# Another order of blocks on TensorE in a fused attention and expert layer: the fourth up block and both shared down products among the scores, three expert products moved

## What is computed

```
xl = layernorm(layernorm(x));  c = layernorm(ctx)            # latents and context
q = xl @ W_q ; k, v = [c ; xl] @ W_kv                         # 4 heads of 64, 333 keys
q, k = rmsnorm(q) * q_gamma / 8, rmsnorm(k) * k_gamma
x1 = x + softmax(mask(q k^T)) v @ W_out + b_out
h  = layernorm(x1)
route: sigmoid(h @ gate^T), the better of 2 groups of 4 experts, its top 2, weights normed, * 2.5
out = x1 + relu(h @ shared_up^T)^2 @ shared_down^T
         + sum over 8 experts of w_e * relu(h @ up_e^T)^2 @ down_e^T
```

## Time and profile before

| what | value |
|---|---|
| median of 3 runs | 1337.84 us (1335.99 to 1338.17) |
| the profiled execution: its own time | 1337.32 us |
| its span, first to last instruction | 1335.5 us |
| mean granted TensorE clock | 0.988 |
| PE busy | 1243.6 us, 93% |
| PEld busy | 1102.9 us, 83% |
| DVE busy | 1036.1 us, 78% |
| ACT busy | 759.3 us, 57% |
| POOL busy | 536.4 us, 40% |

### The profile page before, as it was taken

How to read it: one execution, slowest core, us unless ns; L and a number is a source line. 1 busy time by engine, 2 the same in 40 slices (tenths; PEclk the granted TensorE clock), 3 DMA queues, 4 the chain that set the end, 5 groups by cost and what they waited for, 6 DMA issues and landing times.

```text
span 1335.5 us, 29598 instructions
## 1 busy us (share of the span) xinstructions
PE 1243.6 (93%) x10176; PEld 1102.9 (83%) x10176; DVE 1036.1 (78%) x3561; ACT 759.3 (57%) x1733; POOL 536.4 (40%) x477
## 2 busy tenths in 40 slices
PE   3799999999999999999999999999999999999997
PEld 2588888888888888888888888888888888888886
DVE  3678877778877778877778877778877778877775
ACT  3566555656555656555656555656555656555652
POOL 4234444334444334444334444334444334444332
PEclk9799999999999999999999999999999999999998
DMA  4000000000000000000000000000000000000000
GB/s 141 11 12 20 20 20 19 2 20 20 20 20 19 1 20 20 20 20 20 2 20 20 20 20 19 2 20 20 20 20 20 2 20 20 20 20 19 2 9 17
DMA packets 28228, 25.86 MB, mean 19 GB/s; under 512 B 6640, under 2 KB 27536, under 8 KB 28080
## 3 DMA queue, kind: packets, MB, share of 16 engines
q1 hardware_dynamic: 27744, 23.83, 5.7%
q0 software_dynamic: 336, 0.14, 0.2%
HBM read 15.57 MB, written 8.39 MB: 18 GB/s over the span
## 4 chain that ended last, share of the span: by engine, by line
PE 40%; issue 25%; DVE 13%; ACT 12%; POOL 9%; DMA 1%; DVEq 0%; ACTq 0%; POOLq 0%
PE up_ps L261 6%; PE attn_ps L356 6%; PE up_ps L263 6%; PE up_ps L262 6%; ACT probs L618 5%; PE attn_ps L370 4%; POOL k_scale L1134 4%; ACT relu L663 3%; ACT relu_sb L658 3%; DVE masked L831 3%; POOL ln_lo L1145 3%; DVE acc L997 2%; PE attn_ps L309 2%; PE down_ps L261 2%; PE down_ps L262 2%
## 5 line engine op out<-in xcount | busy, mean ns | idle before, releaser
L1177 POOL TENSOR_TENSOR hid_lo<-relu,hid_hi 128x512 fp32r<-128x512 f32 x192 | 246.9, 1286 | 442.2 <-DVE hid_hi L982 442.2
L261 PE MATMUL down_ps<-down_hi,hid_hi 128*128 128x256 f32 x768 | 234.3, 305 | 14.6 <-issue 12.5
L261 PE MATMUL up_ps<-x_hi,up_hi 128*128 128x256 f32 x768 | 230.0, 299 | 2.7 <-ACT x_hi L647 1.2
L997 DVE SCALAR_TENSOR_TENSOR acc<-down_ps,route_w,acc 128x256 f32<-128x256 f32 x512 | 221.4, 474 | 2.8 <-PE down_ps L263 2.4
L262 PE MATMUL up_ps<-x_lo,up_hi 128*128 128x256 f32 x768 | 216.3, 282 | 0.0
L263 PE MATMUL up_ps<-x_hi,up_lo 128*128 128x256 f32 x768 | 216.3, 282 | 0.0
L263 PE MATMUL down_ps<-down_hi,hid_lo 128*128 128x256 f32 x768 | 215.8, 281 | 0.0
L262 PE MATMUL down_ps<-down_lo,hid_hi 128*128 128x256 f32 x768 | 215.5, 281 | 0.0
L618 ACT ACTIVATE probs<-masked,neg_max,q_scale 128x333 f32<-128x333 f32 x256 | 167.6, 656 | 73.6 <-DVE neg_max L838 73.6
L982 DVE CAST hid_hi<-relu 128x512 fp32r<-128x512 f32 x192 | 124.5, 648 | 83.9 <-ACT relu L663 83.6
L658 ACT ACTIVATE relu_sb<-up_ps 128x512 f32<-128x512 f32 x192 | 114.6, 597 | 129.2 <-PE up_ps L263 123.2
(11 more groups left out here) (147 smaller groups left out, 2820.6 us busy)
## 6 DMA issues: line engine op xcount, KB each, us to landing
x_in<-in_x SPq DMA_DIRECT2D x32, 256.0 KB, 2.8
out<-acc SPq DMA_DIRECT2D x32, 256.0 KB, 2.1
c_in<-in_ctx SPq DMA_DIRECT2D x32, 77.0 KB
up_stage<-in_up_t SPq DMA_DIRECT2D x1, 1536.0 KB, 12.2
down_stage<-in_down_t SPq DMA_DIRECT2D x1, 1536.0 KB, 15.0
mask_in<-in_mask SPq DMA_DIRECT2D x32, 9.6 KB, 2.6
w_stage<-in_w_kv SPq DMA_DIRECT2D x1, 512.0 KB, 5.6
w_stage<-in_w_q SPq DMA_DIRECT2D x1, 256.0 KB, 5.0
```

The lines of the kernel that those rows point to most:

```text
L261: nc.tensor.matmul(out_ap, s_hi, m_hi, start=first, stop=False)
L997: nc.vector.scalar_tensor_tensor(acc[:, t, :], down_ps[:, (e + 1) % 2, t * D:(t + 1) * D], route_w[:, t, e:e + 1], acc[:, t, :], ALU.mult, ...
L1177: nc.gpsimd.tensor_tensor(hid_lo[:, p % HID_RING, :], relu2[:, p % 2, :], hid_hi[:, p % HID_RING, :], ALU.subtract).then_inc(hid_lo_done, 1)
```

## The change

Only the order of calls in three functions `step` is changed; no instruction is added, removed or altered.

TensorE: `up` 3 moves from behind `transpose_probs` 0 to before `score_pair` 2, and `score_pair` 2 to before both `down_shared`, which now follow each other. `down_expert` 5 moves from before `spread_inverse` to behind the first `project_kv`; both `project_out` now follow each other, and the second `project_kv` stands behind them; `down_expert` 7 moves behind `transpose_x2`. VectorE: `add_expert` 5 moves behind both `attn_low`; `layer_norm2` moves before the first `k_norms`, and `normalize2` before the second. GpSimd: `rstd_second` moves before the first `k_scales`. ScalarE's order is the same as before. The code after the last step, which does the experts of batch 31, is not changed.

```diff
--- before.py
+++ after.py
@@ -494,12 +494,12 @@
                 score_pair(b, 0, experts)
                 ffn("up", 2)
                 score_pair(b, 1, experts)
+                ffn("up", 3)
+                score_pair(b, 2, experts)
                 ffn("shared", 0)
-                score_pair(b, 2, experts)
                 ffn("shared", 1)
                 score_pair(b, 3, experts)
                 transpose_probs(b, 0)
-                ffn("up", 3)
                 transpose_probs(b, 1)
                 ffn("down", 0)
                 transpose_probs(b, 2)
@@ -519,21 +519,20 @@
                 transpose_probs(b, 6)
                 ffn("down", 4)
                 transpose_probs(b, 7)
-                ffn("down", 5)
                 spread_inverse(b, following)
                 probs_times_v(b, 3)
                 if following:
                     project_kv(b + 1, 1)
+                ffn("down", 5)
                 project_out(b, 0, following)
+                project_out(b, 1, following)
                 if following:
                     project_kv(b + 1, 2)
-                project_out(b, 1, following)
-                if following:
                     project_kv(b + 1, 0)
                     project_q(b + 1)
                 ffn("down", 6)
+                transpose_x2(b)
                 ffn("down", 7)
-                transpose_x2(b)
@@ -1070,15 +1069,15 @@
                     ln_high(b + 1, False)
                 add(4)
                 attn_out(b, first)
-                add(5)
                 attn_low(b, 0)
                 attn_low(b, 1)
+                add(5)
+                layer_norm2(b, first)
                 if following:
                     k_norms(b + 1, 0, False)
-                layer_norm2(b, first)
+                normalize2(b, first)
                 if following:
                     k_norms(b + 1, 1, False)
-                normalize2(b, first)
                 if following:
                     k_normalize(b + 1, 0, False)
                     k_normalize(b + 1, 1, False)
@@ -1194,9 +1193,9 @@
                 low(5)
                 if following:
                     ln_low(b + 1)
+                rstd_second(b, first)
+                if following:
                     k_scales(b + 1, 0, False)
-                rstd_second(b, first)
-                if following:
                     k_scales(b + 1, 1, False)
```

More of the change, by code:

```diff
@@ L1196, in step @@
                     ln_low(b + 1)
-                    k_scales(b + 1, 0, False)
                 rstd_second(b, first)
                 if following:
+                    k_scales(b + 1, 0, False)
                     k_scales(b + 1, 1, False)
```

## The result

The changed kernel takes 1313.68 us (median of 4 runs, 1312.72 to 1314.18) against 1336.91 for the kernel before on the same chip: a ratio of 0.9825, with a 95% interval of 0.9811 to 0.9839. Forecast were 1310 and the range 1303 to 1322. Sign, range and mechanism held; the gain was 23.2 us where 27.8 were expected.

The account below looks back on a forecast made before the run. PE, 96% busy, was taken as part of a loop bound by a VectorE and GpSimd chain. Terms of 0.88 us a step gave 26.4 over 30 loops, 27.8 with both ends: 1310 us, range 1303 to 1322.

Parts of the forecast that it names:

- The two chains: Whole step: PE is one part of a loop; a VectorE and GpSimd chain sets 18.95 us from `x_lo` to `hid_lo` 3.
- Scores and shared products: Middle of step: PE ready about 1.2 us sooner, but only 0.23 stays at `down_expert` 2, which needs `hid_lo` of pair 3.
- `down_expert` 5: Before the first `project_kv`: taking this product out brings 0.08 us; a wait of about 0.7 stands in its place.
- The end: End of step: second `project_kv` costs 0.62 us more; from it to the end of `x_lo` takes 1.19 less.
- PE at X: Start of step: `up` 0 starts 0.35 us behind the end of `x_lo`, not 0.10; `x_res` covers the lateness.
- rival 1: First casts: chain hangs on PE's `up` 0 through relu and square; 0.63 us a step, about 1317; chance 15%.
- The sum: Per step 0.23 + 0.08 - 0.62 + 1.19 = 0.88 us; 26.4 over 30 loops, 27.8 with step 0 and the last.
- Rival 5: End of kernel keeps full clock, or PE's lead helps a place taken as fixed; 1300 to 1305 us; chance 5%.
- Rival 2: An unseen new wait, likely at `layer_norm2` or `transpose_probs` 2, takes 0.2 to 0.6 us a step; 1316 to 1328; chance 10%.
- Rival 4: Whole step: moved work only moves the waits; time within 0.2% of before; chance 4%.
- Rival 3: End of step: `x_hat` is held by `k_scale` 0 beside it; -0.32 us a step, 1346, slower; chance 6%.
- The row against the rule: `x_hat` took 0.74 us beside `k_scale` 1, unheld, though the skill's rule excludes VectorE in two-port mode beside GpSimd.

Follow-up runs that it names:

- e1: Kernel before with only the middle changed: `up` 3 and `score_pair` 2 before both shared products, end of step as before; 1329.43 us, ratio 0.9934.
- e4: Changed kernel with GpSimd's residual sum `x_res` made in the step before, behind `ln_lo`, in two buffers by turns; 1294.45 us, ratio 0.9668.
- e6: Changed kernel with `down_expert` 5 on TensorE back before `spread_inverse`; 1312.44 us, ratio 0.9823.
- e7: Changed kernel with the second `project_kv` back between the two `project_out`; 1365.54 us, ratio 1.0219.
- e3: Changed kernel with VectorE's and GpSimd's old order at the step's end, except `add_expert` 5; TensorE's order kept; 1348.83 us, ratio 1.0079.
- e2: Changed kernel with scores, `up` 3 and shared products as before, so only the new end of the step; 1321.81 us, ratio 0.9876.
- e9: e8 with GpSimd also holding `hid_lo` of pair 5 and the residual sum until both `at_lo` are done; 1286.13 us, ratio 0.9612.
- e8: e4 with GpSimd's `ln_lo` made before `hid_lo` of pair 5; 1308.21 us, ratio 0.9788.
- e10: Changed kernel with the residual sum as one GpSimd instruction of 128x1024, second half unused; 1323.85 us, ratio 0.9897.
- e5: Changed kernel with GpSimd's residual sum made twice in its place, first into spent staging space; 1324.06 us, ratio 0.9908.

## Why the prediction was right

**The two chains.** That PE at 96% is not the bound by itself, and that the time from X to `down_expert` 2 hangs on VectorE and GpSimd, was the first claim; e1 (0.97 of PE's waits gone, 0.21 gained) and e4 (1.27 of GpSimd's work gone, 0.62 gained) show it.

**Scores and shared products.** Forecast 0.23, measured 0.21, by e1 alone. PE's waits in its place were forecast as 0.3 before `transpose_probs` 2 and 0.4 before `down_expert` 2. The first was 0.27. The second shows as an idle time of only 0.10, but from start to start it is there: the last transposed products start 0.25 ahead of `down_expert` 2 in the kernel before and 0.59 after (634.61 to 635.20), 0.34 more. The row in the kernel before, where `down_expert` 2 starts at 647.01:

```profile
646.76 0.49 PE L356 MATMUL attn_ps<-ident,probs 128*111 128x128 f32 x3
```

The prediction would call itself wrong if X to `down_expert` 2 were not 18.95. It is 19.01 in the mean and 18.99 in the step shown; before, too, the mean (19.22) is 0.04 over the one step that was read (19.18).

**`down_expert` 5.** Forecast 0.08 at the first `project_kv`, measured 0.08. By e6 the move as a whole is a loss: 0.07 gained there, 0.16 lost up to the second `project_kv`. The two waits were given as 0.7 together: 0.14 before `probs_times_v` 3 and 0.36 before `project_kv` were there.

**The end.** Forecast -0.62 and +1.19, measured -0.67 and +1.10. These are the terms that were mis-sized. The 0.05: the first product of `project_kv` takes 0.46 behind its wait, as against 0.40 in a block without one, so the block of 1.40 that I had taken from the earlier trace rows is longer by that much. The 0.09: `k_scale` 0 started at K + 3.20 as said, but takes 1.74 in the mean where 1.64 was counted, and `k_scale` 1 ends at K + 5.91 and not at K + 5.80. Part of this is a slip in the sum, since 3.20 + 1.64 + 1.01 is 5.85. Behind it 1.72 stood for 1.75. Why `k_scale` 0 is longer stays open: in e7 `x_hat` lies beside it too, and it takes 1.64. e3 shows the cause of the term (the order on VectorE and GpSimd), e7 that both `project_out` have to come first for it.

**PE at X.** `up` 0 was put at X + 0.35 and starts at X + 0.11. The blocks ahead of it take less time in the new order than in my count, so the lateness against which rival 1 was weighed was not there.

**The sum.** 0.21 + 0.08 - 0.67 + 1.10 = 0.72 a step for 0.88, which is 4.8 us over 30 loops. The span fell by 1335.5 - 1311.8 = 23.7: 21.7 in the loops, 1.07 in the last step (forecast 0.9), 1.55 before the first X (forecast 0.5), and 0.5 lost behind the last X. Of the 1.55, 0.47 is the order: e2, with the new end and a stretch at half clock as long as before (20.48), has its first X at 66.99 for 67.46. The rest, and what is lost at the end, go with such stretches, which lie differently; the forecast had neither, and half of the one is lost again by the other. Windows at the half clock, start of the kernel before:

```profile
31.59:52.07 20.48, 11.58 (x67) 9.46 (x68) 15.98 (x43) 11.54 (x25) 3.74 (x3) 0.50 0.07 18
```

and of the kernel after, at its start and in its last two stretches:

```profile
31.29:48.36 17.07, 8.17 (x49) 6.79 (x48) 14.67 (x38) 9.43 (x18) 3.69 (x3) 0.50 0.08 22
1280.57:1283.98 3.41, 3.41 (x17) 3.17 (x17) 2.32 (x6) 0.52 (x2) 0.00 (x0) 0.50 0.03 7
1290.81:1294.22 3.41, 2.92 (x14) 2.95 (x15) 2.60 (x10) 0.00 (x0) 0.85 (x2) 0.50 0.00 0
```

The first stretch is 3.41 us shorter. At the end the kernel before has one stretch of 10.24 us, the kernel after two of 3.41, and yet it is not faster there, since one of them falls on the shared products (they start 9.7 behind the last X, after a wait of 3.3, and take 4.2 for 2.9 before). Rival 5, a gain of 5 to 10 us by the clock, did not come. I did not test what moves these stretches.

**The other rivals.** Rival 1 (1317) is wrong for this kernel: e4 shows what held the casts; it came true in e7 alone, at half clock. Rival 2: no new wait took from the gain. The order of `layer_norm2` and the k sum held (k sum at K + 2.22), but with less room than the 0.13 that was counted: `layer_norm2` ends 0.02 before the squares of k are there. Rival 4 is refuted by the result. Rival 3, the slower one, asked whether `k_scale` 0 would hold `x_hat`: it did not, the pair lasts 0.74 before and after (mean of one 411 and 412 ns).

**The row against the rule.** The prediction took `x_hat` for an instruction that a GpSimd sum would hold. No trace shows this. `x_hat` is never beside a sum or a subtraction of GpSimd; and casts and copies take 0.29, 0.32 and 0.42 us for 256, 333 and 512 elements per partition, while the `x_hat` of the first normalisation takes as long for 256 as a cast for 512, with nothing of GpSimd beside it (lines view, after):

```profile
L765 DVE TENSOR_SCALAR x_hat<-x_in,mv,rstd 128x256 f32<-128x256 f32 x64 | 23.5, 411 | 23.2 <-POOL rstd L1133 23.2
```

Whether an inverse root holds less than a sum is better seen at the copy `inv_wide`. Beside `hid_lo` it takes 0.54 to 0.61, with nothing beside it 0.29 (e9, 30 times), and once in each run it lies beside an inverse root (after):

```profile
47.59 0.30 DVE L850 COPY inv_wide<-row_inv 128x256 f32<-128x256 f32 x1
47.55 0.86 POOL L1133 TENSOR_TENSOR rstd<-var,minus_half 128x3 f32<-128x3 f32 x1 [12.54 <-DVE var L758]
```

It is not held, as far as the profile's rough spans on GpSimd tell. The Trainium skill ("SBUF — State Buffer", section "SBUF: two separate sides") has GpSimd exclude a VectorE instruction that is in a two-port mode, or that has two inputs from SBUF while GpSimd reads SBUF, for the whole instruction: the casts, `at_lo` (1.79 for 0.76) and the comparison (1.37 for 0.29) agree, the copy beside the root does not if it runs in such a mode, and `x_hat` decides nothing, since no run shows that it does. Why a root lets the copy through was not tested, and no cast lies beside a root in any run.

## What to carry to other kernels

Where a loop repeats, cut a period at the points where a wait ends last, and sum the terms between them; a wait of the busiest engine is worth only what the term around it shrinks by, here 0.21 of 0.97. Look in the lines for small instructions that take far more time than their size asks for, as the 128x128 comparison with 1.37 us: it lay beside a long GpSimd instruction, and an order that puts the two apart was a gain with no work saved, provided that what is moved doesn't come to lie beside another one, as in e8. When an edit makes one engine's results come sooner, turn the order of the engines that use them as well: here PE's new end without the new order on VectorE and GpSimd was slower than no change at all.

## What the runs showed of the hardware

- Some VectorE instructions that start beside a GpSimd sum or subtraction of 128x512 end only behind it: casts of 128x512 (0.42 becomes 1.04 and 1.35) and subtractions of 128x256 (1.79 for 0.76 in a pair) 0.28 behind, the comparison of 128x128 (1.37 for 0.29) and the copy `inv_wide` (0.54 to 0.61 for 0.29) 0.15 behind, the addition of 128x16 in the router 0.03 behind. The hold grows with the GpSimd instruction (2.38 us in e10), and it ends at an instruction's end even if the next GpSimd instruction is ready (e5).
- Others beside the same `hid_lo` are not held: `add_expert` takes 0.48 in 198 cases beside it and 0.48 in 194 without, the mask addition 0.50 in both, the reciprocal of 128x4 0.17. The first two read one operand from PSUM.
- GpSimd's inverse roots held nothing that lay beside them: `x_hat` has its 0.74 for the pair, `inv_wide` its 0.30, beside a root of 128x3. No cast lay beside one.
- The granted clock fell to 0.50 for 3.41 us at a time in the middle of a kernel whose PE is busy for 97% (e7: 1148.83 of 1185.00), in 19 steps of 29, each right behind the end of a step. In the 10 us before such a stretch PE's longest idle time was 0.33. The changed kernel, with 97.5%, has none, nor has e3 with VectorE's and GpSimd's order of before, though its PE idles more, 1040.76 of 1100 us busy between 100 and 1200 and 1.5 at a time. e7 is 1.6 a step slower than the changed kernel, 0.5 of it by this. What in e7's end brings it on was not tried.
